# Row-maximum products of two heads as two 64-row tiles of TensorE's array, packed at rows 0 and 64

## What is computed

```
xn = layernorm(x)                                       # 2048 x 256
q, k, v = xn @ Wq + bq, xn @ Wk + bk, xn @ Wv + bv      # per head, 16 wide
scores = q @ k.T * 16**-0.5 + causal                    # 1024 x 1024 per head and batch
y = softmax(scores) @ v;   attn = y @ Wo + bo
top2 of xn @ Wr -> softmax gates
ffn = sum over the two experts of gate * ((clip(silu(xn @ Wg), -7, 7) * (xn @ Wu)) @ Wd)
out = x + attn + ffn
```

## Time and profile before

| | before |
|---|---|
| median of three runs | 528.88 us (527.51 to 530.34) |
| the profiled execution | 527.32 us, of which the span from first to last instruction is 525.3 us |
| mean granted TensorE clock | 0.961 of full speed |
| TensorE busy (matmul) | 450.0 us, 86% of the span, 2368 records |
| VectorE busy | 332.4 us, 63% |
| ScalarE busy | 263.8 us, 50% |
| GpSimd busy | 159.6 us, 30% |
| row-maximum products (L1003) | 384, 125.7 us busy, 344 ns each on the mean |
| score products (L1028) | 384, 121.4 us busy, 334 ns |
| V products (L1047) | 768 records, 82.7 us busy |
| maxima on VectorE (L788, L791) | 256 records 124.7 us, 128 records 88.2 us |

### The profile page before, as it was taken

One profiled execution on the slowest core, in us unless ns is written; L12 is line 12 of the kernel. 1 busy time (PEld: TensorE's weight loads), 2 busy tenths in 40 slices (PEclk: granted clock), 3 DMA queues, 4 the chain that ended last, 5 costly groups with the idle time before them and its releaser, 6 DMA issues.

```text
span 525.3 us, 7823 instructions
## 1 busy us (share of the span) xinstructions
PE 450.0 (86%) x2368; PEld 203.5 (39%) x2368; DVE 332.4 (63%) x1023; ACT 263.8 (50%) x646; POOL 159.6 (30%) x198
## 2 busy tenths in 40 slices
PE   1777936987999999999989998899899989998876
PEld 1335612332344344434434444433433343433323
DVE  4585889785867686566665565546655666661671
ACT  1353300665446555564655454554555565656751
POOL 2210007584343233314341242123241333323020
PEclk9998965999799999999999999999999999999997
DMA  7469912587181008101810044001710101100851
GB/s 252 145 131 287 175 30 58 165 281 217 39 153 38 24 23 160 33 22 32 149 40 22 21 90 85 20 21 41 140 42 21 36 26 33 31 12 8 269 167 40
DMA packets 31726, 46.98 MB, mean 89 GB/s; under 512 B 6336, under 2 KB 18753, under 8 KB 31687
## 3 DMA queue, kind: packets, MB, share of 16 engines
q1 hardware_dynamic: 26055, 35.97, 27.9%
q0 software_dynamic: 4768, 9.33, 6.5%
q10 hardware_dynamic: 864, 1.19, 0.8%
HBM read 31.49 MB, written 15.63 MB: 90 GB/s over the span
## 4 chain that ended last, share of the span: by engine, by line
PE 65%; DVE 12%; ACT 7%; issue 6%; POOL 4%; DMA 4%; SPq 1%; POOLq 0%; ACTq 0%
PE ps_w L1085 14%; PE ps_y L1047 12%; PE ps_s L1028 9%; PE ps_s L1003 9%; PE ps_w L1113 7%; POOL slot_values L595 4%; ACT probs L668 4%; PE ps_w L1073 3%; PE ps_w L943 2%; DVE ps_s L788 2%; PE ps_w L967 2%; PE ps_w L1106 2%; DMA packk<-qk_parts 2%; PE ps_w L1080 1%; DVE mxa L791 1%
## 5 line engine op out<-in xcount | busy, mean ns | idle before, releaser
L668 ACT ACTIVATE probs<-ps_s 128x512 f32<-128x512 f32 (+3 forms) x384 | 176.9, 495 | 113.3 <-PE ps_s L1028 112.2
L788 DVE CUSTOM_DVE_ANT_0 ps_s<-ps_s,maskrow 128x128 f32<-128x128 f32 (+3 forms) x256 | 124.7, 500 | 59.6 <-PE ps_s L1003 58.6
L1003 PE MATMUL ps_s<-packk,packq 96*128 96x512 bf16 (+3 forms) x384 | 125.7, 344 | 18.6 <-DVE mxa L791 10.4
L1028 PE MATMUL ps_s<-packq,packk 99*128 99x512 bf16 (+3 forms) x384 | 121.4, 334 | 6.8 <-ACT probs L668 5.2
L791 DVE TENSOR_REDUCE mxa<-ps_s 128x1 f32<-128x512 f32 x128 | 88.2, 689 | 55.9 <-PE ps_s L1003 54.5
L1085 PE MATMUL ps_w<-wgu,xgt 128*128 x156 | 82.8, 613 | 3.3 <-issue 2.0
L1047 PE MATMUL ps_y<-probs,v 128*32 128x512 f32 (+3 forms) x768 | 82.7, 502 | 2.3 <-ACT probs L668 1.6
L610 POOL DMA_INDIRECT expert_rows<-yo,slots x39 | 39.6, 1015 | 125.7 <-ACT yo L706 123.4
L620 POOL TENSOR_SCALAR_AFFINE_SELECT probs<-probs 128x512 f32<-128x512 f32 x64 | 41.9, 654 | 112.0 <-ACT probs L668 111.6
L1028 PEld LDWEIGHTS ps_s<-packq,packk 99*128 99x128 bf16 x384 | 36.6, 98 | 91.6 <-ACT probs L668 55.0
L1003 PEld LDWEIGHTS ps_s<-packk,packq 96*128 96x128 bf16 x384 | 38.3, 100 | 64.0 <-issue 19.3
(11 more groups left out here) (107 smaller groups left out, 395.0 us busy)
## 6 DMA issues: line engine op xcount, KB each, us to landing
qk_parts<-stage SPq DMA_DIRECT2D x24, 256.0 KB, 3.4
wgu<-in_wgu SPq DMA_DIRECT2D x8, 512.0 KB
stage<-expert_rows SPq DMA_DIRECT2D x16, 256.0 KB, 3.8
packq<-qk_parts SPq DMA_DIRECT2D x8, 384.0 KB, 5.3
packk<-qk_parts SPq DMA_DIRECT2D x8, 384.0 KB, 7.2
x<-in_x SPq DMA_DIRECT2D x4, 512.0 KB, 8.5
xn_rows<-probs SPq DMA_DIRECT2D x4, 512.0 KB, 9.2
packq<-qk_parts SPq DMA_DIRECT2D x8, 256.0 KB, 7.9
```

What stands on the lines that cost most here:

```text
L668: act.activation(probs[:, g % 2, h, 0:width], ps_s[:, score_bank(k), 0:width], ACT.Exp, scale=SCALE)\
L788: ins = dve.tensor_tensor_reduce(out=chunk, in0=chunk, in1=maskrow[:, BANK - width:], scale=1.0, scalar=NEG, op0=ALU.add, op1=ALU.max, acc ...
L1003: pe.matmul(ps_s[:, SCORE_RING + n % NAT_RING, 0:width], packq[0:MAXROW, u % SLOTS, h, P * i:P * (i + 1)], packk[0:MAXROW, u % SLOTS, h, B ...
L1028: pe.matmul(ps_s[:, score_bank(k), 0:width], packk[0:KROWS, u % SLOTS, h, P * j:P * (j + 1)], packq[0:KROWS, u % SLOTS, h, t0:t0 + width], ...
```

## The change

Three things are changed.

- **Pairs.** The chunks of two heads stand alternately in CHUNKS, and `natural` does nothing for an odd chunk and two products for an even one: one on rows 0 to 63 for the even head, one on rows 64 to 111 for the odd head, into two neighbouring banks of the ring. Each takes only the leading part products (LEAD): of six, the even head four, the odd head three. The wait is for both banks: the chunk two before the pair's first must have been reduced. VectorE's stages stay at their places in the plan and its operations are as many as before; the maxima of a head go to another column (`by_pair`).
- **Packs.** The heads of a unit stand in two layouts. The even heads keep 96 rows and 3 more (99 in the score product). The odd heads have their leading parts at row 64, the others at rows 0 to 47, negative maxima at 48 to 50 and zeros to row 63, so that their score product has 112 rows.
- **DMAs.** A unit's load is 12 DMAs of two heads each, not 6 of four heads; the negative maxima of a unit are 6 DMAs, not 3; at the start the rows of ones are two DMAs and the zero rows two more, and GpSimd sets 32 rows to zero ahead of the ones.

The diff, cut to its core:

```diff
-RUNS = ((0, 0, 0, 3), (3 * HD, 1, 0, 2), (5 * HD, 2, 0, 1))
-MAXROW = 6 * HD
-KROWS = MAXROW + PARTS
+PAIR = 2
+RUNS = (((0, 1, 0, 2), (2 * HD, 2, 0, 1), (3 * HD, 0, 0, 3)),
+        ((64, 1, 0, 2), (64 + 2 * HD, 2, 0, 1), (0, 0, 0, 3)))
+LEAD = (slice(0, 64), slice(64, 64 + 3 * HD))
+MAXROW = (6 * HD, 3 * HD)
+KROWS = (6 * HD + PARTS, 64 + 3 * HD)
...
-CHUNKS = [(h, i, s) for h in range(UH) for i in range(TB) for s in range(i * P // BANK + 1)]
+CHUNKS = [(h, i, s) for h0 in range(0, UH, PAIR) for i in range(TB) for s in range(i * P // BANK + 1)
+          for h in range(h0, h0 + PAIR)]
...
-                for row, *first, length in RUNS:
-                    for op, pack in enumerate((packq, packk)):
-                        src = qk_d[op, grp, first[op]:first[op] + length, :, h0:h0 + UH, T * b:T * b + T]
-                        sp.dma_start(pack[row:row + HD * length, u % SLOTS, :, :],
-                                     src.rearrange("r d h t -> (r d) h t")).then_inc(pack_in[u % SLOTS], 16)
+                for which in range(PAIR):
+                    for row, *first, length in RUNS[which]:
+                        for op, pack in enumerate((packq, packk)):
+                            src = qk_d[op, grp, first[op]:first[op] + length, :, h0 + which:h0 + UH:PAIR, T * b:T * b + T]
+                            sp.dma_start(pack[row:row + HD * length, which, u % SLOTS, :, :],
+                                         src.rearrange("r d h t -> (r d) h t")).then_inc(pack_in[u % SLOTS], 16)
...
-                for part in range(PARTS):
-                    dst = packq[MAXROW + part:MAXROW + part + 1, u % SLOTS, :, :]
-                    sp.dma_start(dst.rearrange("o h (i t) -> o (h i) t", t=P),
-                                 negt[32 * part:32 * part + 32, :]).then_inc(neg_in[u % SLOTS], 16)
+                rows = EACH * TB
+                for which in range(PAIR):
+                    for part in range(PARTS):
+                        at = MAXROW[which] + part
+                        dst = packq[at:at + 1, which, u % SLOTS, :, :]
+                        begin = UH * TB * part + rows * which
+                        sp.dma_start(dst.rearrange("o h (i t) -> o (h i) t", t=P),
+                                     negt[begin:begin + rows, :]).then_inc(neg_in[u % SLOTS], 16)
...
-                if n >= NAT_RING:
-                    pe.wait_ge(max_done, n - NAT_RING + 1)
-                pe.matmul(ps_s[:, SCORE_RING + n % NAT_RING, 0:width], packq[0:MAXROW, u % SLOTS, h, P * i:P * (i + 1)],
-                          packk[0:MAXROW, u % SLOTS, h, BANK * s:BANK * s + width], start=True, stop=True)\
-                  .then_inc(nat_ready, 1)
+                if n + PAIR > NAT_RING:
+                    pe.wait_ge(max_done, n + PAIR - NAT_RING)
+                for which in range(PAIR):
+                    pe.matmul(ps_s[:, SCORE_RING + (n + which) % NAT_RING, 0:width],
+                              packq[LEAD[which], which, u % SLOTS, h // PAIR, P * i:P * (i + 1)],
+                              packk[LEAD[which], which, u % SLOTS, h // PAIR, BANK * s:BANK * s + width],
+                              start=True, stop=True).then_inc(nat_ready, 1)
...
-                pe.matmul(ps_s[:, score_bank(k), 0:width], packk[0:KROWS, u % SLOTS, h, P * j:P * (j + 1)],
-                          packq[0:KROWS, u % SLOTS, h, t0:t0 + width], start=True, stop=True).then_inc(scores_ready, 1)
+                rows = slice(0, KROWS[h % PAIR])
+                pe.matmul(ps_s[:, score_bank(k), 0:width], packk[rows, h % PAIR, u % SLOTS, h // PAIR, P * j:P * (j + 1)],
+                          packq[rows, h % PAIR, u % SLOTS, h // PAIR, t0:t0 + width], start=True, stop=True).then_inc(scores_ready, 1)
```

39 lines of the change are left out of this document (28 added, 11 removed).

## The result

| | before | changed |
|---|---|---|
| median of 4 runs | 528.21 us (527.51 to 530.34) | 541.39 us (539.34 to 545.50) |
| ratio, with its 95% interval | | 1.025 (1.018 to 1.032) |
| the profiled execution | 527.32 us, span 525.3 | 541.33 us, span 539.1 |
| mean granted TensorE clock | 0.961 | 0.962 |

The changed kernel is slower, by 2.5%. The forecast was 537.5 us, and the range of 515 to 547 holds the result. The mean clock is the same, so what follows is told in work and waits first; where half-clock stretches differ, it is said.

A forecast was written before the change was run, and what follows sets the result against it. TensorE was taken to bound the kernel. Pair switching, the three-bank ring, an earlier second product and a later start summed to +8.8 us, 536.1 by the profiled execution's own time; forecast median 537.5 us, range 515 to 547.

The forecast's parts named there:

- The nearest change of shape in the old trace: TensorE around the product with V, four 32-column tiles: 0.09 us going in, about 0.10 out; 0.095 taken per 64-row switch.
- I had held this open: Rival for TensorE's pairs: both tiles run one after the other, 0.333 + 0.177 us a pair, about 558 us; chance 0.16.

The follow-up runs named there:

- pair_order: Kernel before with the row-maximum products of two heads together and one wait for both banks, full 96-row products, old packs and DMAs: 534.54 us, 1.012.
- own_waits_full: Kernel before with the paired order, full 96-row products, old packs and DMAs, each product waiting for its own bank alone: 529.84 us, 1.002.

## What to carry to other kernels

Two switches of 0.10 us eat nearly all that a lone pair of 512-column products saves (0.22 us) and more than all that shorter ones save, so count the changes of shape in TensorE's queue, in the stage that matters, before the columns. By these prices tiles would pay where several pairs follow one another; that is an estimate from the 0.22 and the 0.10, and no kernel here has such an order. The nearest change of shape in the old trace gave their price. Before moving work to save switches, look at which waits the old places filled: a control with the new places and the old products tells the two apart, and here it was the places that lost 45 us. And before a term of 2 us is read from one profile, look at the same row in the profiles of kernels that didn't change there.

## What the runs showed of the hardware

- A 64-row tile behind a full-array product, and the other way round, costs 0.10 us at 2.4 GHz, and so does a 64-row tile ahead of a 32-column tile. Products of 96, 99, 112 and 115 rows follow one another at the bare stream (0.22 us for 512 columns).
- Two 64-row tiles that write different PSUM banks over the same 128 partitions run wholly side by side, 3 ns apart. I had held this open, since the V product's tiles write different partitions.
- Loads of 384, 256 and 128 KB or twice as many of 192, 128 and 64 KB, in pieces of 2 KB: no difference that a run could tell (1.000, 0.998 to 1.003). Six small DMAs in place of three behind one another on a queue did put off the first product that needs them, by 1.3 us.
- The same indirect DMA of the placement took 3.04 to 5.89 us in the profiles of eleven kernels, with no tie to the kernel's time.
- A common wait for two banks of three costs 1% of this kernel (pair_order against own_waits_full), although it holds one product of 0.17 us back by one maximum.
